# Windowed attention on one core: attend in 32x64 tiles of four stacked heads instead of 64x64 tiles of two

## The chip, the core and the metric

One NeuronCore of a Trainium2 chip runs the whole program in one launch. The metric is the device time of that launch in microseconds (us); the median of three runs is quoted. Engines are named as in the profile: PE (TensorE: matrix products, with PEld its weight loads), DVE (VectorE), ACT (ScalarE), POOL (GpSimd) and SP (SyncE, which here only issues DMAs).

## The reference

Two blocks work on `x` of 8 batches x 256 positions x 128 channels. The first block (linear attention, mixture of experts, a thresholded attention) is called the early part here. The change is in the second block's feed-forward place, a stack of six transformer layers with windowed attention; cut to what matters:

```python
DIM, DEPTH, HEADS, DIM_HEAD, WINDOW = 128, 6, 16, 64, 32
def attn_layer(x, Wqkv, qs, ksc, Wo):
    q, k, v = jnp.split(x @ Wqkv, 3, -1)          # each 256 x (16 heads x 64)
    q, k = l2norm(q) * qs, l2norm(k) * ksc        # then rotated by position
    out = local_attention(q, k, v)
    return out @ Wo
def local_attention(q, k, v):                     # 8 windows of 32 rows
    # keys and values of a window: the window before it and its own, 64 in all
    sim = einsum('bhwie,bhwje->bhwij', bq, bk2) * 8.0
    mask = (it < jb) | (it > jb + 32) | (jb == -1)
    attn = softmax(where(mask, -max, sim), -1)
    return einsum('bhwij,bhwje->bhwie', attn, bv2)
for i in range(DEPTH):
    x = attn_layer(shift_tokens(x), ...) + x
    x = ffn_layer(shift_tokens(x), ...) + x       # LayerNorm, gated gelu 128 -> 2 x 341 -> 128
```

## The kernel before

The six layers are 48 units `u` (layer `u // 8`, batch `u % 8`), each a generator `late(u)` in every engine's program. A table of slots per engine (`PE_AT`, `ACT_AT`, `DVE_AT`, `POOL_AT`, `SP_AT`) says at which slot after the start of its unit a step is written; units start 32 slots apart (`LATE_SPACING`), and `interleave` merges them. The tables set only the order in which instructions stand on an engine: engines run their lists in order and wait on semaphores. Five to seven units are in flight at once. The early part has tables of the same kind.

A unit has two chunks `c` of 128 positions. Its steps, with the lines of the profile:

- Projections: PE multiplies the shifted input by `Wqkv` in 12 pieces of 512 columns, 3 products each (L724 to L726, high and low parts in fp32r). ACT copies q and k to `raw` (L1063) and v to `vn` (L1080).
- Norm and rotation: ACT squares (L1071), DVE sums (L1528), ACT takes the root (L1137, L1138), POOL multiplies by the cosine (L1734) and adds (L1743), DVE multiplies by the sine (L1541) and normalises (L1549). PE transposes (L747), ACT copies to `qT` (L1091) and `kT` (L1097).
- Scores: `scores(c, half)` writes the mask with a bf16 product (L760), then 32 fp32 products in each half (L769) on 64-row, 32-column tiles: contraction over 64 head channels, 32 queries of one window as weights, 64 keys moving. One pair of PSUM banks, `s_pair`, serves both chunks in turn. In the trace each fp32 product is two load-and-multiply pairs, so a half is 64 records.
- Softmax: DVE takes the maximum and subtracts it (L1561, L1562), ACT the exponential (L1104), DVE sum, reciprocal and scaling (L1569 to L1571). PE transposes (L781), ACT copies to `pT` (L1111), so that the 64 keys of one head and window lie on 64 partitions, two heads on 128.
- Attend: `attend(c, half)` on 64x64 tiles (L799): 64 keys contracted, 64 value channels as weights, 32 queries moving, 128 records for each chunk. Results go to a second pair of banks, `o_pair`, which ACT copies to `oT` (L1119).
- Values: since a window needs the window before it, SP writes `vn` to HBM (L1883) and reads it back as `v2`, paired, each block twice (L1891).
- After it: output product `wo` (L882), residual (DVE L1609), LayerNorm (PE L887 and L891, ACT L1207 to L1213, DVE L1614 to L1624), the up products (L816 to L818), gelu (ACT L1129, with a table load of its own), gate (DVE L1578), down product (L904), residual (DVE L1631).

Three PSUM banks rotate among the remaining products, and a fourth holds tables of the rotation and small vectors.

## Time and profile before

| | |
|---|---|
| median of 3 runs | 1952.4 us (1951.92 to 1953.56) |
| span of the profiled execution | 1955.3 us |
| busy, of that span | PE 95%, PEld 80%, DVE 81%, ACT 81%, POOL 55% |
| mean granted TensorE clock | 0.979 of full speed |
| DMA | 212.35 MB, mean 109 GB/s |

The profile gives no time for the profiled execution beside its span. All times in the rows are of that one execution, 2.9 us above the median. The early part runs until about 430 us, and the 48 units follow, the first ones overlapped with its end. Within the units the work repeats, so one unit is read closely and multiplied; a row of the timeline gives the start, the time to the end of the last of its instructions, and how many were merged. The duration of a product holds its way through the array, so what it occupies is read from start to start.

### The profile page before, as it was taken

What the parts mean: (1) busy time and instruction counts of PE and PEld (TensorE: products, weight loads), DVE (VectorE), ACT (ScalarE), POOL (GpSimd) and SP (SyncE); (2) the same over time, 40 slices, a digit from 0 to 9 for tenths busy, and PEclk for the clock granted to TensorE, in tenths of its full rate; (3) what the DMA queues carried; (4) which work ended last, traced back from release to release, by engine and by line L of the source; (5) the groups of instructions that cost most, each with busy time, mean ns of one, the idle gap of its engine ahead of it and who ended that gap; (6) DMA issues with size and microseconds to landing.
All of it is one profiled execution on the core that took longest, in us unless ns stands there. A gap on an engine that the chain in (4) does not pass through costs nothing.

```text
span 1955.3 us, 77164 instructions
## 1 busy us (share of the span) xinstructions
PE 1866.8 (95%) x34029; PEld 1568.0 (80%) x34029; DVE 1587.6 (81%) x2234; ACT 1592.8 (81%) x2751; POOL 1069.6 (55%) x523
## 2 busy tenths in 40 slices
PE   6899999878999999999999999999999999999987
PEld 4788989856878888888878888887888888888876
DVE  3566765478898988989888998988898998989873
ACT  2578878667988888898988889897888889888864
POOL 3333222176565666657566666756575666657530
PEclk7999999979999999999999999999999999999998
DMA  6333322023335343353434443444434344333341
GB/s 175 121 127 124 105 80 66 2 72 96 105 99 156 96 132 111 105 150 95 124 100 130 123 125 108 112 122 122 113 103 132 97 137 129 105 115 94 101 105 29
DMA packets 134183, 212.35 MB, mean 109 GB/s; under 512 B 26871, under 2 KB 51034, under 8 KB 133850
## 3 DMA queue, kind: packets, MB, share of 16 engines
q1 hardware_dynamic: 133676, 207.36, 37.0%
q8 instruction: 269, 4.41, 1.0%
q14 instruction: 64, 0.52, 0.1%
q10 hardware_dynamic: 174, 0.05, 0.0%
HBM read 136.76 MB, written 70.60 MB: 106 GB/s over the span
## 4 chain that ended last, share of the span: by engine, by line
PE 86%; ACT 6%; DVE 5%; issue 3%; DMA 0%; ACTq 0%; SPq 0%; DVEq 0%
PE o_pair L799 9%; PE bank L747 9%; PE bank L882 9%; PE s_pair L769 7%; PE bank L724 7%; PE bank L725 6%; PE bank L726 6%; PE bank L781 4%; PE bank L649 4%; PE bank L904 3%; PE bank L816 2%; PE bank L817 2%; PE bank L818 2%; PE bank L887 2%; PE s_pair L760 1%
## 5 line engine op out<-in xcount | busy, mean ns | idle before, releaser
L1734 POOL TENSOR_TENSOR rt<-raw,rot 128x1024 f32<-128x1024 f32 x192 | 456.3, 2377 | 353.5 <-PE bank L747 328.8
L1743 POOL TENSOR_TENSOR rt<-rt,t 128x2048 f32<-128x2048 f32 x96 | 439.5, 4578 | 178.7 <-DVE t L1541 175.1
L724 PE MATMUL bank<-wqkv,xs 128*128 128x512 f32 x576 | 257.4, 447 | 11.6 <-ACT vn L1080 6.7
L1063 ACT ACTIVATE raw<-bank 128x512 f32<-128x512 f32 x384 | 223.2, 593 | 28.2 <-PE bank L726 14.9
L1528 DVE TENSOR_REDUCE bank<-t 128x32 f32<-128x2048 f32 x96 | 219.7, 2289 | 17.1 <-ACT t L1071 12.6
L726 PE MATMUL bank<-wqkv,xs 128*128 128x512 f32 x576 | 229.9, 399 | 0.0
L725 PE MATMUL bank<-wqkv,xs 128*128 128x512 f32 x576 | 229.8, 399 | 0.0
L747 PE MATMUL bank<-const,rt 128*128 128x128 f32 x1536 | 219.8, 281 | 9.5 <-issue 3.2
L799 PEld LDWEIGHTS o_pair<-pT,v 64*64 64x64 f32 x12288 | 196.2, 135 | 40.3 <-ACT oT L1119 17.6
L1541 DVE TENSOR_TENSOR t<-raw,bank 128x1024 f32<-128x1024 f32 x192 | 225.0, 1213 | 0.6
L1549 DVE TENSOR_TENSOR rt<-rt,bank 128x2048 f32<-128x2048 f32 x96 | 219.6, 2288 | 3.3
L799 PE MATMUL o_pair<-pT,v 64*64 64x32 f32 x12288 | 213.4, 220 | 6.5 <-issue 4.7
L1561 DVE TENSOR_REDUCE sm<-s_pair 128x16 f32<-128x1024 f32 x96 | 117.5, 1224 | 118.9 <-PE s_pair L769 118.2
L747 PEld LDWEIGHTS bank<-const,rt 128*128 128x128 f32 x1536 | 169.5, 142 | 38.6 <-ACT kT L1097 12.9
L1097 ACT ACTIVATE kT<-bank 128x512 f32<-128x512 f32 x192 | 109.2, 594 | 102.6 <-PE bank L747 100.6
L1071 ACT ACTIVATE t<-raw 128x2048 f32<-128x2048 f32 x96 | 184.0, 1917 | 10.4 <-POOL rt L1743 8.5
L769 PEld LDWEIGHTS s_pair<-kT,qT 64*32 64x32 f32 x12288 | 135.1, 106 | 52.4 <-issue 41.8
L882 PE MATMUL bank<-oT,wo 128*128 128x256 f32 x768 | 173.7, 379 | 0.4 <-DVE hh L1578 0.4
L769 PE MATMUL s_pair<-kT,qT 64*32 64x64 f32 x12288 | 167.1, 226 | 6.0 <-issue 6.0
L882 PEld LDWEIGHTS bank<-oT,wo 128*128 128x128 f32 x768 | 145.4, 190 | 22.0 <-DVE hh L1578 0.7
L1091 ACT ACTIVATE qT<-bank 128x512 f32<-128x512 f32 x192 | 113.9, 594 | 41.4 <-PE bank L747 40.3
L724 PEld LDWEIGHTS bank<-wqkv,xs 128*128 128x128 f32 x576 | 110.3, 191 | 34.7 <-ACT vn L1080 7.6
(403 smaller groups left out, 4157.5 us busy)
## 6 DMA issues: line engine op xcount, KB each, us to landing
v<-v_rows SPq DMA_DIRECT2D x288, 256.0 KB, 4.4
v_rows<-vn SPq DMA_DIRECT2D x192, 256.0 KB, 3.7
v<-v_rows SPq DMA_DIRECT2D x96, 192.0 KB, 3.2
w_parts<-wqkv SPq DMA_DIRECT2D x30, 512.0 KB, 3.8
wqkv<-w_parts SPq DMA_DIRECT2D x30, 512.0 KB, 4.1
wraw<-in_L_ffn_Wqkv_dram SPq DMA_DIRECT2D x36, 256.0 KB, 3.1
w_parts<-wqkv SPq DMA_DIRECT2D x10, 341.0 KB, 3.7
w<-w_parts SPq DMA_DIRECT2D x10, 341.0 KB, 5.7
```

Source lines behind the costliest of these rows:

```text
L724: pe.matmul(bank[:, :], hi, w[:, 0, :], start=True, stop=False)
L725: pe.matmul(bank[:, :], hi, w[:, 1, :], start=False, stop=False)
L726: return pe.matmul(bank[:, :], lo, w[:, 0, :], start=False, stop=True)
L747: e = pe.transpose(bank[:, i * P:(i + 1) * P], k.rt_r[c][:, at:at + P], k.ident)
L769: e = pe.matmul(k.s_pair[WIN * g:WIN * (g + 1), at:at + 2 * WIN], qT[rows, hp, WIN * g:WIN * (g + 1)], k.kT[rows, hp, k0:k0 + 2 * WIN], st ...
L799: e = pe.matmul(k.o_pair[cols, at:at + WIN], k.v2_r[c][rows, g, hp * DH:(hp + 1) * DH], k.pT_r[c][rows, hp, WIN * g:WIN * (g + 1)], start= ...
L882: e = pe.matmul(bank[:, 0:S], k.wo[:, n, :], k.oT_r[u % 2][:, n, :], start=(n == 0), stop=(n == INNER // P - 1))
L1063: act.activation(k.raw_r[c][:, n * 512:(n + 1) * 512], k.one.at["qk", j][:, :], ACT.Copy)\
L1528: dve.tensor_reduce(k.rn_p[c], heads(k.t2[:, :]), AX.X, ALU.add).then_inc(s["sq_sum"], 1)
L1541: e = dve.tensor_tensor(pairs(k.t2[:, part]), pairs(k.raw_r[c][:, part])[:, :, ::-1, :], sinv, ALU.mult)
L1734: e = pool.tensor_tensor(heads(k.rt_r[c][:, part]), heads(k.raw_r[c][:, part]), cosv, ALU.mult)
L1743: pool.tensor_tensor(k.rt_r[c][:, :], k.rt_r[c][:, :], k.t2[:, :], ALU.add).then_inc(s["rot_add"], 1)
```

## The change

**Attend.** Weights are now one block of 32 keys x 64 value channels, tiles have 32 rows x 64 columns, and four heads' key blocks are stacked on the four row groups, with two heads beside each other in columns: eight tiles. A value block of window `w` is loaded once and its product moves 64 queries, those of window `w` (the block is their own) and `w + 1` (the block is their previous one), accumulating in PSUM. Per unit there are 128 products as before (256 records), 224 of whose records move 64 columns and 32 move 32, all in one block after both chunks' softmax.

**Keys by block parity.** `kT` holds even blocks, then odd ones, so ACT's copy becomes two instructions of 256 columns. The two 32-key halves of a row of scores are placed by parity, `p` is laid out as window, head, key, and the mask and its spreading matrix follow.

**PSUM.** `so_pair[c]` takes the scores of chunk `c` and then half of the outputs of all 256 positions. Attend waits until DVE has read both pairs, and scores of the next unit wait until ACT has copied the outputs of that pair.

**DMA.** Values are stored in 2 writes per unit (4 before) and read in 8 reads of 128 KB (8 of 192 or 256 KB before). `wo` is loaded without rearranging channels.

**Slots.** All tables are new, also those of the early part, on slots an eighth as long.

```diff
 
-        def attend(c, half):
-            v = 2 * u + c
-            if half == 0:
-                if v:
-                    pe.wait_ge(s["oT"], v)
-                else:
-                    claim(k.banks[6:8])
-                pe.wait_ge(s["pT"], 2 * v + 2)
-                pe.wait_ge(s[f"v2_{c}"], pair_count(v))
-            for m in range(2 * half, 2 * half + 2):
-                for g in range(NW):
-                    for odd, cols in enumerate(halves):
-                        for r, rows in enumerate(halves):
-                            hp, at = 2 * m + odd, r * 512 + m * P + g * WIN
-                            e = pe.matmul(k.o_pair[cols, at:at + WIN], k.v2_r[c][rows, g, hp * DH:(hp + 1) * DH],
-                                          k.pT_r[c][rows, hp, WIN * g:WIN * (g + 1)], start=True, stop=True)
-            if half == 1:
-                e.then_inc(s["pe_o"], 1)
+        def attend():
+            pe.wait_ge(s["smax"], 2 * u + 2)
+            pe.wait_ge(s["pT"], 4 * u + 4)
+            pe.wait_ge(s[f"vq{u % 2}"], value_loads(u))
+            for w in range(NWS):
+                q0, n = w * WIN, 2 * WIN if w + 1 < NWS else WIN
+                for g2 in range(2):
+                    for hq in range(4):
+                        rows, pair = slice(32 * hq, 32 * (hq + 1)), k.so_pair[hq // 2]
+                        at = hq % 2 * 512 + g2 * S + q0
+                        for odd, cols in enumerate(halves):
+                            g = 2 * g2 + odd
+                            e = pe.matmul(pair[cols, at:at + n], k.vq_r[u % 2][rows, w, g, :],
+                                          k.pT[rows, 2 * g + w % 2, q0:q0 + n],
+                                          start=(w == 0 and g2 == 0), stop=(w == NWS - 1), skip_group_check=True)
+            e.then_inc(s["pe_o"], 1)
 
         def up(j):
...
-        def scores(c, half):
+        def scores(c):
             v = 2 * u + c
-            qT = k.qT_r[c]
-            if half == 0:
-                if v:
-                    pe.wait_ge(s["smax"], v)
-                else:
-                    claim(k.banks[4:6])
-                    pe.wait_ge(s["cst"], 1)
-                for r, rows in enumerate(halves):
-                    pe.matmul(k.s_pair[:, r * 512:(r + 1) * 512], k.spread_b[rows, :],
-                              k.mask_b[rows, min(c, 1), :].unsqueeze(1).to_broadcast([DH, HP, 2 * WIN]),
-                              start=True, stop=False, skip_group_check=True)
-                pe.wait_ge(s["qkT"], QK_EVACS * (v + 1))
-            for hp in range(4 * half, 4 * half + 4):
+            qT, pair = k.qT_r[c], k.so_pair[c]
+            if u == 0:
+                claim(k.banks[4 + 2 * c:6 + 2 * c])
+                pe.wait_ge(s["cst"], 1)
+            else:
+                pe.wait_ge(s["oT"], 2 * u - 1 + c)
+            for r, rows in enumerate(halves):
+                pe.matmul(pair[:, r * 512:(r + 1) * 512], k.spread_b[rows, min(c, 1), :],
+                          k.mask_b[rows, :].unsqueeze(1).to_broadcast([DH, HP, 2 * WIN]),
+                          start=True, stop=False, skip_group_check=True)
+            pe.wait_ge(s["qkT"], QK_EVACS * (v + 1))
+            for hp in range(HP):
                 for g in range(NW):
-                    k0 = c * P + g * WIN
+                    even, odd = (NW * c + g) // 2, NWS // 2 + (NW * c + g + 1) // 2
                     for r, rows in enumerate(halves):
                         at = r * 512 + hp * 2 * WIN
-                        e = pe.matmul(k.s_pair[WIN * g:WIN * (g + 1), at:at + 2 * WIN],
-                                      qT[rows, hp, WIN * g:WIN * (g + 1)], k.kT[rows, hp, k0:k0 + 2 * WIN],
+                        e = pe.matmul(pair[WIN * g:WIN * (g + 1), at:at + 2 * WIN],
+                                      qT[rows, hp, WIN * g:WIN * (g + 1)], k.kT[rows, hp, even:odd + 1:odd - even, :],
                                       start=False, stop=True, skip_group_check=True)
-            if half == 1:
-                e.then_inc(s["pe_s"], 1)
+            e.then_inc(s["pe_s"], 1)
 
         def transpose_p(c, n):
             v = 2 * u + c
+            p = k.p_r[c][:, :, :, :].rearrange("p w n j -> p w (n j)")
             bank = one_bank_for(("pT", 2 * v + n), "pT", 2 * v + n + 1)
...
-            act.activation(k.kT[:, 4 * (n - 2):4 * (n - 2) + 4, WIN + c * P:WIN + (c + 1) * P], src, ACT.Copy)\
-                .then_inc(s["qkT"], 1)
+            kT = k.kT[:, 4 * (n - 2):4 * (n - 2) + 4, :, :]
+            src = parity(src)
+            even, odd = 2 * c, NWS // 2 + 1 + 2 * c
+            for w, at in enumerate((even, odd)):
+                e = act.activation(kT[:, :, at:at + 2, :], src[:, :, w, :, :], ACT.Copy)
+            e.then_inc(s["qkT"], 1)
...
 
-        def evacuate_o(c):
-            v = 2 * u + c
-            act.wait_ge(s["pe_o"], v + 1)
-            if c == 0 and u >= 2:
+        def evacuate_o(n):
+            act.wait_ge(s["pe_o"], u + 1)
+            if n == 0 and u >= 2:
                 act.wait_ge(s["pe_wo"], u - 1)
-            act.activation(k.oT_r[u % 2][:, :, c * P:(c + 1) * P], k.o_pair[:, :].rearrange("p (n i) -> p n i", i=P),
+            act.activation(k.oT_r[u % 2][:, 4 * n:4 * n + 4, :], k.so_pair[n][:, :].rearrange("p (n i) -> p n i", i=S),
                            ACT.Copy).then_inc(s["oT"], 1)
...
-        def store_values(c, r):
+        def store_values(c):
+            if c == 0 and u >= 2:
+                sp.wait_ge(s[f"vq{u % 2}"], value_loads(u - 2))
+            sp.wait_ge(s["vn"], 4 * u + 2 * c + 2)
+            sp.dma_start(k.v_rows[u % 2, c * P:(c + 1) * P, :], k.vn_r[c][:, :, :, :].rearrange("p q g d -> p (q g d)"))\
+                .then_inc(s[f"st_v{c}"], 16)
+
+        def load_values(c, r):
+            if r == 0:
+                sp.wait_ge(s[f"st_v{c}"], 16 * (u + 1))
             if c == 0 and r == 0 and u >= 2:
-                for n in range(TC):
-                    sp.wait_ge(s[f"v2_{n}"], pair_count(2 * (u - 2) + n))
-            sp.wait_ge(s["vn"], 4 * u + 2 * c + r + 1)
-            sp.dma_start(k.v_rows[u % 2, c * P:(c + 1) * P, r, :], k.vn_r[c][:, r * 512:(r + 1) * 512])\
-                .then_inc(s[f"st_v{c}"], 16)
-
-        def pair_values(c, half):
-            v = 2 * u + c
-            if half == 0:
-                sp.wait_ge(s[f"st_v{c}"], 32 * (u + 1))
-                if u:
-                    sp.wait_ge(s["pe_o"], v - 1)
-                else:
-                    sp.wait_ge(s["zero_kv"], ZEROS)
-            g0 = 1 if c == 0 and half == 0 else 0
-            first = (NW * c + g0 - 1 + half) * WIN
-            for r in range(2):
-                at = 2 * WIN * r + WIN * half
-                src = k.v_rows[u % 2, first:first + (NW - g0) * WIN, r, :].rearrange("(g j) e -> j g e", j=WIN)
-                sp.dma_start(k.v2_r[c][at:at + WIN, g0:, :], src).then_inc(s[f"v2_{c}"], 16)
+                sp.wait_ge(s["pe_o"], u - 1)
```

The order on PE around the mask, scores and attend. In these rows a product stands once for its two records, `bank` is a rotating bank, L781 the transposes of probabilities, L904 the down product, L891 the LayerNorm variance. Before:

```order
L781 MATMUL bank<-const,p 128x128 x8
L904 MATMUL bank<-hh,w 128x256 x3
L760 MATMUL s_pair<-mask_b,spread_b 128x512 x2
L769 MATMUL s_pair<-kT,qT 32x64 x32
L891 MATMUL bank<-lnf,ones_d 128x256
L724 MATMUL bank<-wqkv,xs 128x512
L725 MATMUL bank<-wqkv,xs 128x512
L726 MATMUL bank<-wqkv,xs 128x512
L799 MATMUL o_pair<-pT,v 64x32 x64
L724 MATMUL bank<-wqkv,xs 128x512
```

After (L751 transposes q and k, L763 is the mask, L772 scores, L801 attend, L728 to L730 projections, L874 the variance):

```order
L751 MATMUL bank<-const,rt 128x128 x8
L801 MATMUL so_pair<-pT,vq 64x64 x112
L801 MATMUL so_pair<-pT,vq 64x32 x16
L728 MATMUL bank<-wqkv,xs 128x512
L729 MATMUL bank<-wqkv,xs 128x512
L730 MATMUL bank<-wqkv,xs 128x512
L728 MATMUL bank<-wqkv,xs 128x512
L729 MATMUL bank<-wqkv,xs 128x512
L730 MATMUL bank<-wqkv,xs 128x512
L874 MATMUL bank<-lnf,ones_d 128x256
L763 MATMUL so_pair<-mask_b,spread_b 128x512 x2
L772 MATMUL so_pair<-kT,qT 32x64 x64
```

Attend was three blocks per unit (32, 32 and 64 products), scores were four halves; now attend is one block of 128 and scores are two blocks of 64.

The order on DVE from the end of the second softmax sum. Before:

```order
L1569 TENSOR_REDUCE sm1<-p1 128x16
L1570 RECIPROCAL bank3<-sm1 128x16
L1571 TENSOR_TENSOR p1<-p1,bank3 128x2x8x64
L1614 TENSOR_TENSOR lnf<-xf0,bank0 128x256
L1561 TENSOR_REDUCE sm0<-s_pair 128x16
L1562 TENSOR_TENSOR p0<-s_pair,sm0 128x2x8x64
L1547 COPY bank3<-rn0 128x32
L1549 TENSOR_TENSOR rt0<-rt0,bank3 128x2048
L1528 TENSOR_REDUCE bank3<-t2 128x32
L1530 TENSOR_SCALAR rn1<-bank3 128x32
```

After (L1555 to L1557 is the softmax sum, L1600 the centring of LayerNorm, L1533 and L1535 normalise, L1514 and L1516 sum the squares `t2`, L1527 multiplies by the sine, L1606 to L1610 finish LayerNorm, L1547 takes the maximum of the next unit):

```order
L1555 TENSOR_REDUCE sm1<-p1 128x16
L1556 RECIPROCAL bank3<-sm1 128x16
L1557 TENSOR_TENSOR p1<-p1,bank3 128x1024
L1600 TENSOR_TENSOR lnf<-xf0,bank2 128x256
L1533 COPY bank3<-rn0 128x32
L1535 TENSOR_TENSOR rt0<-rt0,bank3 128x2048
L1514 TENSOR_REDUCE bank3<-t2 128x32
L1516 TENSOR_SCALAR rn1<-bank3 128x32
L1527 TENSOR_TENSOR t2<-raw1,bank3 128x1024 x2
L1606 SCALAR_TENSOR_TENSOR bank1<-lnf,cols,bank1 128x256
L1609 TENSOR_SCALAR hn<-bank1,cols 128x256
L1610 SCALAR_TENSOR_TENSOR hn<-bank1,cols,hn 128x256
```

The maximum of the next unit stood right behind the centring. Now normalise, the sum of squares, the rotation and the end of LayerNorm stand between them.

The order on ACT around the probabilities' copies. Before:

```order
L1207 ACTIVATE lnf<-lnf 128x256
L1063 ACTIVATE raw1<-bank0 128x512
L1063 ACTIVATE raw1<-bank1 128x512
L1071 ACTIVATE t2<-raw1 128x2048
L1111 ACTIVATE pT1<-bank2 128x512
L1111 ACTIVATE pT1<-bank0 128x512
L1119 ACTIVATE oT1<-o_pair 128x8x128
L1211 ACTIVATE lnf<-bank2,eps_ln 128x256
L1213 ACTIVATE bank2<-lnf 128x256
```

After (L1076 copies `qT`, L1100 `pT`, L1054 squares, L1086 copies `kT`, L1194 and L1198 belong to LayerNorm, L1107 copies `oT`):

```order
L1076 ACTIVATE qT1<-bank0 128x512
L1100 ACTIVATE pT<-bank1 128x4x128
L1100 ACTIVATE pT<-bank0 128x4x128
L1100 ACTIVATE pT<-bank1 128x4x128
L1100 ACTIVATE pT<-bank2 128x4x128
L1054 ACTIVATE t2<-raw1 128x2048
L1086 ACTIVATE kT<-bank0 128x4x64 x2
L1194 ACTIVATE lnf<-lnf 128x256
L1086 ACTIVATE kT<-bank1 128x4x64 x2
L1107 ACTIVATE oT0<-so_pair0 128x1024
```

The square of the second chunk stood ahead of that unit's pair of `pT` copies; now it stands behind four of them.

## Rows read from the trace of the kernel before

**Rows 1.** Busy time of each engine in two neighbouring stretches of 30.70 us (windows view).

```profile
core 0: us, PE busy (x) PEld busy (x) DVE busy (x) ACT busy (x) POOL busy (x), PEclk, DMA share, GB/s
1239.80:1270.50 30.70, 30.70 (x657) 25.56 (x652) 27.95 (x32) 27.38 (x47) 19.98 (x9) 1.00 0.44 117
1270.50:1301.20 30.70, 30.70 (x656) 25.57 (x649) 27.94 (x33) 27.38 (x47) 19.96 (x9) 1.00 0.36 101
```

**Rows 2.** Shares of the chain that ended last, by engine (the page).

```profile
PE 86%; ACT 6%; DVE 5%; issue 3%; DMA 0%; ACTq 0%; SPq 0%; DVEq 0%
```

**Rows 3.** Timeline of ACT: first exponential of the first and of the last unit.

```profile
429.77 1.04 ACT L1104 ACTIVATE p<-p 128x1024 f32<-128x1024 f32 x1
1900.93 1.04 ACT L1104 ACTIVATE p<-p 128x1024 f32<-128x1024 f32 x1
```

**Rows 4.** Timeline: where DVE and ACT sit idle within one undisturbed unit, idle in brackets.

```profile
1279.33 1.23 DVE L1561 TENSOR_REDUCE sm<-s_pair 128x16 f32<-128x1024 f32 x1 [2.04 <-PE s_pair L769]
1298.73 2.29 DVE L1528 TENSOR_REDUCE bank<-t 128x32 f32<-128x2048 f32 x1 [0.16 <-ACT t L1071]
1290.71 0.60 ACT L1091 ACTIVATE qT<-bank 128x512 f32<-128x512 f32 x1 [0.75 <-PE bank L747]
1294.26 1.09 ACT L1097 ACTIVATE kT<-bank 128x512 f32<-128x512 f32 x2 [1.61 <-PE bank L747]
```

**Rows 5.** Timeline of PE: two of the three attend blocks and what follows each.

```profile
1281.21 1.14 PE L799 MATMUL o_pair<-pT,v 64*64 64x32 f32 x64
1282.27 0.39 PE L816 MATMUL bank<-hn,w 128*128 128x256 f32 x1
1300.73 2.07 PE L799 MATMUL o_pair<-pT,v 64*64 64x32 f32 x128
1302.73 0.50 PE L724 MATMUL bank<-wqkv,xs 128*128 128x512 f32 x1
```

**Rows 6.** Timeline of PE: mask product, half a score block, and what follows.

```profile
1291.04 0.39 PE L760 MATMUL s_pair<-mask_b,spread_b 64*128 64x512 bf16 x2
1291.36 0.86 PE L769 MATMUL s_pair<-kT,qT 64*32 64x64 f32 x64
1292.17 0.67 PE L887 MATMUL bank<-xf,ones_d 128*128 128x256 f32 x2
```

**Rows 7.** Timeline of PE: a full-array product run, what follows, and column-tiled products.

```profile
1286.57 3.62 PE L882 MATMUL bank<-oT,wo 128*128 128x256 f32 x16
1290.03 1.08 PE L747 MATMUL bank<-const,rt 128*128 128x128 f32 x8
164.87 1.08 PE L568 MATMUL bank<-e_kp,e_vext 128*32 128x128 f32 x32
```

**Rows 8.** Groups by line: ACT copies of 512 and of 256 columns out of PSUM.

```profile
L1097 ACT ACTIVATE kT<-bank 128x512 f32<-128x512 f32 x192 | 109.2, 594 | 102.6 <-PE bank L747 100.6
L1031 ACT ACTIVATE e_hr<-bank 128x256 f32<-128x256 f32 x7 | 2.6, 372 | 0.0
```

**Rows 9.** Timeline of DVE: second softmax sum, LayerNorm centring, maximum, normalise.

```profile
1290.56 1.21 DVE L1569 TENSOR_REDUCE sm<-p 128x16 f32<-128x1024 f32 x1
1293.24 0.42 DVE L1614 TENSOR_TENSOR lnf<-xf,bank 128x256 f32<-128x256 f32 x1
1293.67 1.22 DVE L1561 TENSOR_REDUCE sm<-s_pair 128x16 f32<-128x1024 f32 x1
1296.07 0.18 DVE L1547 COPY bank<-rn 128x32 f32<-128x32 f32 x1
```

**Rows 10.** Timeline of ACT: square, transposed probabilities, table load, gelus.

```profile
1296.79 1.91 ACT L1071 ACTIVATE t<-raw 128x2048 f32<-128x2048 f32 x1
1298.61 1.06 ACT L1111 ACTIVATE pT<-bank 128x512 f32<-128x512 f32 x2
1282.34 1.28 ACT L1129 ACT_TABLE_LOAD   x1
1283.64 1.19 ACT L1129 ACTIVATE hh<-bank,cols 128x256 f32<-128x256 f32 x3
```

## What the change was predicted to do

> **What bounds the kernel now.** I read the busy time in two neighbouring stretches first. Each stretch of 30.70 us holds one unit's work: 656 or 657 multiplies, 32 or 33 DVE and 47 ACT instructions. PE is busy in all 30.70 us at the full clock, DVE in 27.95, ACT in 27.38, POOL in 19.98 [rows 1]. The chain that ended last agrees, with 86% on PE [rows 2]. The pace over the whole stack comes from the first exponential of the first and of the last unit: (1900.93 - 429.77) / 47 = 31.30 us for a unit [rows 3]. So an undisturbed unit takes 30.70 us by PE, and 0.60 us on average is disturbance, above all at the changes of layer, where DVE makes new rotation tables.
>
> How near the next engine is matters as much. In one unit DVE waited 2.04 us for PE's scores and 0.16 us for ACT's square, so DVE alone needs 30.70 - 2.20 = 28.5 us. ACT waited 0.75 and 1.61 us for transposes, so it needs 28.3 us [rows 4]. A saving on PE is worth its full size for 2.2 us a unit at most, and nothing after that.
>
> **Attend.** Two blocks of 64 records take 1282.27 - 1281.21 = 1.06 us each and one of 128 takes 1302.73 - 1300.73 = 2.00 us, 4.12 us a unit or 15.6 to 16.6 ns a record [rows 5]. What should a record cost in the new form? Sixteen records of 256 columns on the full array took 1290.03 - 1286.57 = 3.46 us, 216 ns each or 0.84 ns a column [rows 7]. A 32-column record thus streams for 27 ns. With four tiles side by side 16 ns a record is 64 ns a tile, so 37 ns beside the streaming are spent on weights and handing over. A score record streams 64 columns, 54 ns; 64 of them took 1292.17 - 1291.36 = 0.81 us, 12.7 ns each, on eight tiles 101 ns a tile, so 47 ns beside the streaming [rows 6]. The new record has the scores' 64 moving columns and eight tiles, and attend's 64-column weights. Streaming 54 plus 37 to 47 gives 91 to 101 ns a tile, over eight tiles 11.4 to 12.7 ns a record, for 256 records 2.9 to 3.2 us. I take 3.0, near the score row, whose tile count it shares: a gain of 1.1 us. The ends are streaming alone (256 x 54 / 8 = 1.7 us, gain 2.4) and the old price (4.1 us, no gain). A third bound lies above it: if only the four row groups work beside each other, see the rivals.
>
> **Scores.** The products are the same, but in two blocks, not four halves. Joining two attend blocks saved 2 x 1.06 - 2.00 = 0.12 us [rows 5], so two joins give 0.24, the lower bound. The half block's 12.7 ns a record holds entry and exit, while streaming needs 6.8, so up to 1 us is possible; I take 0.4. Between the blocks PE changes its tile shape seven times a unit now, and three times after; no row prices a change by itself, and the 0.12 us of a join is the nearest, so I put 0.3 us on four changes fewer (bounds 0 and 4 x 0.12 = 0.5). The mask product stays at 1291.36 - 1291.04 = 0.32 us [rows 6]. PE then needs 30.7 - 1.1 - 0.4 - 0.3 = 28.9 us a unit, with 27.0 and 30.4 as ends.
>
> **What ACT and DVE gain or lose.** Each of the four `kT` copies of 512 columns (594 ns) becomes two of 256. The nearest 256-column copy out of PSUM took 372 ns [rows 8], so a copy grows by at most 2 x 372 - 594 = 150 ns, a unit by 0.6 us, less where starts overlap. ACT needs 28.3 + 0.3 to 0.6, say 28.8 us. The value copies and `oT` copies move the same columns. DVE's softmax reads and writes the same 1024 elements in another order with runs of 32; I put nothing on it (bounds: nothing and, were runs to matter, some tenths). DVE stays at 28.5. POOL has 10 us to spare. Three engines now need 28.5 to 28.9 us: the bound is no longer one engine, it is their hand-overs.
>
> **The hand-overs.** Two are visible in the order. First, ACT's square of the second chunk stood ahead of the `pT` copies and now stands behind four of them, which wait for DVE's second softmax sum. DVE does centring and normalise after that sum and then needs this square. From the end of the sum: PE's last eight transposes, 1.0 us; the last copy, about 0.5 of the 1.06 for two, plus latency, 0.8; then the square, 1.91: 3.7 us [rows 10]. DVE meanwhile has 1293.67 - 1293.24 = 0.43 us of centring and 2.5 us of normalise (1296.07 to 1298.73 less the 0.16 idle) [rows 4, 9], so it waits 0.8 to 0.9 us where it waited 0.16. Second, gelu needs a table load of 1.28 us and 1.19 us for its three parts [rows 10], behind copies of projections, and DVE's gates come after only one maximum and subtraction (1296.07 - 1293.67 = 2.40 us [rows 9]); I put 0.2 us on it (0 to 0.7). DVE's 28.5 plus 0.9 plus 0.2 is 29.6 us. PE at 28.9 hides below that, which is why attend's price matters little unless it comes out above 3.7 us.
>
> The shared PSUM closes a ring: scores, both maxima, exponentials, both sums, transposes, attend, `oT` copy, scores. On DVE, all but five steps lies between the first maximum and the end of the second sum: centring 0.43, one normalise 2.5, one sum of squares 2.3 [rows 4, 9], one rotation (two passes over 1024, like the maximum's 1.22 each) and LayerNorm's end (three of about 0.45, like the centring), 9.0 us. That leaves 28.5 - 9.0 = 19.5 us. Then come PE's transposes and the copy (1.8), attend (3.0), two projections and the variance (eight records at about 0.22, 1.7 [rows 7]), and mask with scores (1.8): 27.8 us [rows 5, 6, 10]. It is shorter than 29.6, so it doesn't bind by this count, with 1.8 us in hand.
>
> **Values by DMA.** The value traffic halves, at a DMA share of 0.36 to 0.44 [rows 1]. DMA has no share in the chain [rows 2], so nothing is gained. The reads sit about a unit ahead of their attend in SP's list, and two buffers alternate by unit; I put 0 on them. The other loads that SP's list moved past them (weights of the next layer, `wo`) keep their order relative to their readers.
>
> **Sum.** A unit goes from 30.7 to 29.6 us undisturbed, and I leave the 0.60 us of disturbance: fewer transfers help, but DVE's layer tables now meet an engine without slack. 47 x 1.1 = 52 us. The early part's new tables and the ends of the stack I put at nothing (some us either way; no row prices them). On the profiled span that is 1955.3 - 52 = 1903, and 2.9 us less on the scale of the median: **1901 us**.
>
> **Rivals.**
> - Hand-overs vanish in queues that run ahead, and attend costs 2.5 us or less: a unit takes 28.6 us, 47 x 2.1 = 99 us, **1854 us**. For it: gaps in rows 4 were few. Against: three engines with 0.3 us of slack each. 17%.
> - Attend keeps its price of 16 ns a record (4.1 us), since weights and hand-over and not tiles set it. PE then needs 30.0, a unit 30.3 with hand-overs: 19 us, **1934 us**. For it: 37 of the 64 ns a tile are not streaming. 15%.
> - The ring binds, on the other side. Its place is the one wait of attend for both chunks and the wait of scores for the `oT` copy. Its 27.8 us plus waits inside it (residual behind `wo`, gates behind gelu, the copy queued behind the square) pass the present 30.7 when they reach 2.9 us; at 3.3 us the unit takes 31.1 and the kernel **1971 us**. Against: the waits I can name in it come to about 1. 8%.
> - Only row groups work side by side. What the rows show: 32 records of 128 columns on four column tiles took 1.08 us, 34 ns each, where streaming alone is 108 ns a tile [rows 7], so column tiles do overlap; and with two row groups an attend record at 27 ns of weights and 27 ns of streaming would cost 27 ns, not 16 [rows 5]. Were it so, 256 records at (27 + 54) / 4 ns would take 5.2 us, PE 31.1, the kernel **1971 us**. 3%. The Trainium skill says it, in "TensorE: Matmul & The Clock Gate", Part 3 on packing: a weight load overlaps a running multiply only where the row groups differ. By that rule as it stands the change loses; the trace of before disagrees with it for column tiles, so the row decides.
> - The change shifts nothing measurable, because another bound replaces attend exactly: **1952 us**. 2%.
>
> **How the numbers follow.** The forecast case (a unit of 29.1 to 30.1 us, 1877 to 1924 us) has 55%. The range goes from just above the first rival's value to just above the second's: 1855 to 1938 us, which leaves out the slow rivals, the null case and part of the first. Within 0.2% (4 us) is about what this measurement can't tell from no change. Faster is 55 + 17 + 15 = 87%, same 2%, slower 8 + 3 = 11%.
>
> **What would show it.** In the profile after: attend's block of 256 records from start to start (3.0 us; 4.1 or 5.2 by the rivals); the stretch of one unit near 29.6 us with DVE busy 28 of it, ACT about 28, and PE no longer waited on by DVE's maximum; DVE idle near 0.9 us before the sum of squares, released by ACT's square; the `kT` copies near 370 ns. A wait of scores on the `oT` copy of over 1 us each unit would mean that the ring binds. PE busy throughout at over 30 us would mean that attend was not made cheaper. The number is wrong if the disturbances grow, or if the early part moved by more than 10 us.

## The result and the profile after

The changed kernel takes **2130.65 us** (median of 4 runs, 2123.47 to 2138.64), the kernel before beside it 1952.16 us. The ratio is **1.090** (95% interval 1.086 to 1.094): 9% slower, where 1901 us were forecast and 1938 us was the upper end. The profiled execution took 2123.47 us, its span is 2122.1 us.

The page of the kernel after: busy time (share of the span) and instructions, the instruction queue, and the chain that ended last.

```profile
PE 1872.4 (88%) x34029; PEld 1544.8 (73%) x34029; DVE 1590.1 (75%) x2234; ACT 1594.3 (75%) x2943; POOL 1066.0 (50%) x521
q8 instruction: 269, 4.41, 0.9%
PE 58%; ACT 18%; DVE 12%; issue 11%; POOL 1%; DMA 0%; ACTq 0%; SPq 0%; DVEq 0%; POOLq 0%
```

PE is still 58% of the chain, but it was 86% [rows 2], and 11%, where it was 3%, are now "issue": time in which an engine stood still and waited for nothing that the profile shows. The first exponential of the first and of the last unit (timeline of ACT, kernel after) answer to [rows 3]:

```profile
463.97 1.04 ACT L1093 ACTIVATE p<-p 128x1024 f32<-128x1024 f32 x1
2069.63 1.06 ACT L1093 ACTIVATE p<-p 128x1024 f32<-128x1024 f32 x1
```

So the first unit comes 464.0 - 429.8 = 34 us later, and a unit takes (2069.6 - 464.0) / 47 = 34.16 us in place of 31.30, which is 134 us over the stack. What follows the last exponential is 2 us shorter. 34 + 134 - 2 is the 167 us between the two spans.

Where a unit's time went is read at attend. Timeline of PE, kernel after; it answers to [rows 5]:

```profile
1303.69 1.95 PE L801 MATMUL so_pair<-pT,vq 32*64 32x64 f32 x162
1307.73 1.55 PE L801 MATMUL so_pair<-pT,vq 32*64 32x64 f32 x94 [2.09 <-issue]
1309.20 0.80 PE L728 MATMUL bank<-wqkv,xs 128*128 128x512 f32 x1
...
1337.69 1.87 PE L801 MATMUL so_pair<-pT,vq 32*64 32x64 f32 x153
1341.37 1.51 PE L801 MATMUL so_pair<-pT,vq 32*64 32x64 f32 x103 [1.81 <-issue]
```

The records run at the forecast price, and then PE stands still for about 2 us in the middle of the block. In the next unit the gap is 9 records earlier. Behind it stands a second cost: the projection's first matmul takes 0.80 us. The windows view of the kernel after shows why, in its column PEclk (the granted clock, 1.00 is full; the columns are those of [rows 1]). The fourth row is the middle of the stack, the last one a unit that stays at the full clock:

```profile
1305.70:1307.70 2.00, 0.00 (x0) 0.00 (x0) 2.00 (x1) 1.17 (x5) 1.92 (x2) 1.00 0.00 0
1307.70:1309.30 1.60, 1.57 (x95) 1.51 (x94) 1.57 (x4) 0.00 (x0) 1.05 (x1) 0.61 0.05 10
1309.30:1311.10 1.80, 1.80 (x5) 1.42 (x6) 0.99 (x1) 1.02 (x1) 0.67 (x1) 0.50 0.00 0
700.00:1900.00 1200.00, 1088.63 (x22631) 884.76 (x22634) 984.83 (x1122) 963.34 (x1752) 697.56 (x281) 0.95 0.27 80
...
1117.20:1149.80 32.60, 30.04 (x646) 24.55 (x645) 28.06 (x32) 27.59 (x52) 19.97 (x8) 1.00 0.23 67
```

PE is empty for 2.00 us, and then the clock falls to 0.50. Added up over the stack's 47 units, the trace has 40 such stretches with 160 us at half clock (before: 4 with 17 us). A stretch at half clock gives back half of its length at most: 160 / 2 / 47 = 1.7 us a unit. Neighbouring units give the likelier size: with a gap of 1.6 to 1.8 us in both, one at the full clock takes 32.3 us (from 1598.8) and the next, with one such stretch, 33.7 (from 1631.1). With 40 stretches, some of them longer, in 47 units that is an estimate of 1.2 us a unit.

The waits view of the kernel after, 700 to 1900 us (35 units): waiter, releaser, us in total, times, longest.

```profile
PE so_pair L801 <- issue: 73.4, 37, 3.9
ACT oT L1107 <- PE so_pair L801: 80.3, 35, 4.4
DVE bank L1606 <- ACT bank L1200: 102.7, 36, 5.7
DVE hh L1564 <- ACT hh L1117: 53.0, 35, 1.9
DVE bank L1514 <- ACT t L1054: 31.0, 35, 1.1
```

The gap costs 73.4 / 35 = 2.1 us a unit. ACT waits for the end of attend 2.3 us a unit, and DVE then 2.9 us for ACT. The gap and the clock are 3.3 of the 34.16 us, 3.8 at most. That leaves 30.4 to 30.9 us where the forecast had 30.2. The unit at the full clock says the same: 32.6 us less its gap of 1.6 us is 31.0, no shorter than an undisturbed unit before (30.7).

Over 38 or 39 units in the middle of the stack, the mean time from each group of matmuls to the start of the next (us a unit, added up from the trace's records; waits and half clock are in it, a wait in the row of the group that stands ahead of it):

| | before | after | attend halved | attend cut in 3 |
|---|---|---|---|---|
| attend | 4.34 | 5.39 | 1.65 | 4.26 |
| projection products | 9.08 | 10.88 | 10.62 | 10.56 |
| scores | 3.34 | 3.50 | 3.39 | 3.94 |
| all else | 14.59 | 14.54 | 14.62 | 14.26 |
| unit | 31.35 | 34.31 | 30.28 | 33.02 |

The third and the fourth column are experiments `half` and `sp9` below.

### The profile page after: what moved, and what is told of

It is laid out like the page before. It is cut to its first block, busy times and chain, and to the rows that moved or that the text cites. A ratio compares the mean times of both kernels' runs of the same rounds, so it can differ in the third digit from the quotient of the medians.

```text
span 2122.1 us, 77095 instructions
## 1 busy us (share of the span) xinstructions
PE 1872.4 (88%) x34029; PEld 1544.8 (73%) x34029; DVE 1590.1 (75%) x2234; ACT 1594.3 (75%) x2943; POOL 1066.0 (50%) x521
## 4 chain that ended last, share of the span: by engine, by line
PE 58%; ACT 18%; DVE 12%; issue 11%; POOL 1%; DMA 0%; ACTq 0%; SPq 0%; DVEq 0%; POOLq 0%
PE so_pair L801 7%; PE bank L751 6%; PE bank L728 6%; PE bank L865 6%; PE bank L730 4%; PE bank L729 4%; PE bank L786 3%; PE so_pair L772 3%; PE bank L653 3%; ACT L911 3%; ACT L1117 3%; ACT raw L1046 2%; ACT t L1054 2%; DVE bank L1514 2%; DVE t L1527 2%
## 5 line engine op out<-in xcount | busy, mean ns | idle before, releaser
L728 PE MATMUL bank<-wqkv,xs 128*128 128x512 f32 x576 | 289.9, 503 | 32.7 <-ACT vn L1063 15.2
L801 PE MATMUL so_pair<-pT,vq 32*64 32x64 f32 (+1 forms) x12288 | 161.0, 238 | 102.7 <-issue 102.4
L1514 DVE TENSOR_REDUCE bank<-t 128x32 f32<-128x2048 f32 x96 | 219.7, 2289 | 42.0 <-ACT t L1054 42.0
L730 PE MATMUL bank<-wqkv,xs 128*128 128x512 f32 x576 | 243.8, 423 | 0.1
L729 PE MATMUL bank<-wqkv,xs 128*128 128x512 f32 x576 | 242.4, 421 | 0.0
L1535 DVE TENSOR_TENSOR rt<-rt,bank 128x2048 f32<-128x2048 f32 x96 | 219.7, 2288 | 19.8 <-POOL rt L1727 17.5
L801 PEld LDWEIGHTS so_pair<-pT,vq 32*64 32x64 f32 x12288 | 147.9, 137 | 118.3 <-issue 118.3
L1527 DVE TENSOR_TENSOR t<-raw,bank 128x1024 f32<-128x1024 f32 x192 | 224.8, 1212 | 0.6
L751 PE MATMUL bank<-const,rt 128*128 128x128 f32 x1536 | 205.5, 277 | 0.4 <-ACT raw L1046 0.4
L751 PEld LDWEIGHTS bank<-const,rt 128*128 128x128 f32 x1536 | 175.1, 141 | 28.1 <-ACT raw L1046 0.7
L728 PEld LDWEIGHTS bank<-wqkv,xs 128*128 128x128 f32 x576 | 115.5, 200 | 106.3 <-ACT vn L1063 35.1
L1054 ACT ACTIVATE t<-raw 128x2048 f32<-128x2048 f32 x96 | 183.0, 1906 | 6.5 <-POOL rt L1727 5.4
L1107 ACT ACTIVATE oT<-so_pair 128x1024 f32<-128x1024 f32 x96 | 98.4, 1025 | 118.5 <-PE so_pair L801 118.5
L772 PEld LDWEIGHTS so_pair<-kT,qT 64*32 64x32 f32 x12288 | 133.3, 108 | 33.5 <-issue 33.2
L772 PE MATMUL so_pair<-kT,qT 64*32 64x64 f32 x12288 | 150.9, 232 | 6.0 <-issue 5.9
L1606 DVE SCALAR_TENSOR_TENSOR bank<-lnf,cols,bank 128x256 f32<-128x256 f32 x48 | 23.5, 489 | 154.4 <-ACT bank L1200 154.4
L730 PEld LDWEIGHTS bank<-wqkv,xs 128*128 128x128 f32 x576 | 117.6, 204 | 29.7 <-issue 1.5
```

Of the source, the lines that this page charges most:

```text
L728: pe.matmul(bank[:, :], hi, w[:, 0, :], start=True, stop=False)
L729: pe.matmul(bank[:, :], hi, w[:, 1, :], start=False, stop=False)
L730: return pe.matmul(bank[:, :], lo, w[:, 0, :], start=False, stop=True)
L751: e = pe.transpose(bank[:, i * P:(i + 1) * P], k.rt_r[c][:, at:at + P], k.ident)
L772: e = pe.matmul(pair[WIN * g:WIN * (g + 1), at:at + 2 * WIN], qT[rows, hp, WIN * g:WIN * (g + 1)], k.kT[rows, hp, even:odd + 1:odd - even, :],
L801: e = pe.matmul(pair[cols, at:at + n], k.vq_r[u % 2][rows, w, g, :], k.pT[rows, 2 * g + w % 2, q0:q0 + n], start=(w == 0 and g2 == 0), sto ...
```

## What the gap is

**Theory (supply).** PE's instructions reach it in packets, and the new block uses them up faster than they come. Three numbers of the traces speak for it before any experiment:

- The instruction queue brought 269 packets of 16 KB. PE executed 34029 weight loads, 34029 matmuls and 863 semaphore instructions, 68921 in all: 269.2 times 256. So the queue carries PE's program, 256 instructions or 128 records to a packet.
- The shortest distance between two packets' starts is 3.2 to 3.4 us in every one of the 14 kernels of this study.
- Numbered from PE's first instruction, **each of the 50 gaps over 1 us inside attend ends at an instruction whose number leaves 193 or 194 when divided by 256**. A unit has 1299 to 1302 instructions, about 5 x 256 + 20: so the boundary drifts by some 20 instructions, 10 records, a unit, and the two timelines show 9.

If so, gap = 3.4 us less the time in which a packet is used up. In attend 128 records go in about 1.4 us, so the gap should be 2.0 us; it is 2.09 and 1.81 above. What repeats is the time from the first instruction of one packet to the first of the next across a gap: 3.1 to 3.8 us at three gaps in four, 3.5 in the middle. The packets themselves need not stand close: the one ahead of the gap's had come 3.3 to 19 us earlier. So the next packet seems to be sent for only when PE enters the one before it. Six of the 50 gaps are longer than this allows (over 4 us from packet to packet); why is open. The Trainium skill has the store behind this, in "Advanced Engine Details and Errata", section "ISA Cache": a cache line is 16 KB and 256 instructions, and there are "Only 2 cache lines!". The traces agree: if two packets were there at the start, the one that starts last before a gap is the one whose first instruction ends the gap, 2.3 to 2.9 us later, and no packet starts earlier than some 300 instructions ahead of its own, as it would with one line in use and one being filled. The same list of the Trainium skill gives TensorE 128 KB, which would be eight lines; nothing here shows a supply that far ahead.

**Rivals.** *Tile*: 32x64 tiles or four stacked heads are slow in themselves, or collide in a bank. *Hand-over*: the engines' order around attend is what costs, and the gap is only where it shows. *Early slots* for the 34 us.

## Experiments

**half**: one line, every second value window left out, so that attend has 128 records and its outputs lack half of their terms.

```diff
-            for w in range(NWS):
+            for w in range(0, NWS, 2):
```

> The changed kernel computing only the even value windows of attend (64 matmuls, 128 records in place of 256; the odd windows' part of every output is left out), all else as it is. Supply theory: 128 records take 1.4 us at 10.6 ns each, the hole behind them mostly goes (under 0.5 us a unit on average), the clock stays full; unit 34.2 - 1.35 (records) - 2.1 (hole) - up to 1.6 (clock), so 29.2 to 31 us, time 1900 to 1980. If only the records count: 34.2 - 1.35 = 32.8 us a unit, 2065 us. If another engine or the order of the hand-overs binds: 33.5 or more, over 2095 us.

One run: **1942.4 us** (before: 1953.4). Timeline of PE, and the same stretch of windows as above, then the page's packets:

```profile
1184.04 1.59 PE L801 MATMUL so_pair<-pT,vq 32*64 32x64 f32 x128
1185.56 0.51 PE L728 MATMUL bank<-wqkv,xs 128*128 128x512 f32 x1
...
700.00:1900.00 1200.00, 1126.79 (x20544) 897.08 (x20543) 1101.55 (x1263) 1073.63 (x1956) 768.97 (x307) 1.00 0.29 88
...
q8 instruction: 221, 3.62, 0.8%
```

A record in the new tiles costs 1.52 / 128 = 11.9 ns with entry and exit. Undisturbed units take 29.6 us and the mean is 30.24 (1890.3 less 469.1, over 47): taking 1.4 us of records out won 3.9 us. The clock is back at 1.00, with 2 half-clock stretches in place of 40. (27885 + 27885 + 863) / 256 = 221.2, again the packets. A pure count of records would have given 32.8 us a unit. So the records were not slow, which speaks against *tile*; and ACT's wait for attend fell from 80.3 us to 1.9 us in all. But with the missing records put back, 29.6 + 1.4 = 31.0 us, this is no faster than before either: what the whole block would take without its gap no run shows, and the rows leave 29.8 (PE's busy time, see below) to 31.0 us.

**dup**: the kernel **before**, its old 64x64 tiles, with the second chunk's attend issued twice.

```diff
-            for m in range(2 * half, 2 * half + 2):
+            for m in range(2 * (half % 2), 2 * (half % 2) + 2):
...
         yield from t.to("a11")
+        attend(1, 2)
+        attend(1, 3)
         attend(1, 1)
```

> The kernel before with the 64 attend matmuls of the second chunk issued twice in a row (same outputs; 256 records in one run in place of 128, old tile shape 64x64, at 15.6 ns a record in the trace of before). Supply theory: 256 records would take 4.0 us at their own price; a hole of 0.5 to 2 us appears in many of the blocks at a place that drifts by a fixed number of records a unit, a half clock behind some; unit 31.3 + 2.0 + 0.5 to 2.5, 33.8 to 35.8 us, time 2070 to 2165. Tile theory: no hole, exactly +2.0 us a unit, time 1952 + 96 = 2048 us or less.

One run: **2145.8 us**. Timeline of PE in two units:

```profile
1274.29 2.07 PE L799 MATMUL o_pair<-pT,v 64*64 64x32 f32 x128 [0.41 <-issue]
1278.31 0.83 PE L799 MATMUL o_pair<-pT,v 64*64 64x32 f32 x42 [1.95 <-issue]
...
1412.24 2.76 PE L799 MATMUL o_pair<-pT,v 64*64 64x32 f32 x174
1416.30 1.47 PE L799 MATMUL o_pair<-pT,v 64*64 64x32 f32 x82 [1.30 <-issue]
```

The old tiles get the gap as soon as 256 records stand in a row. 128 old records take 2.0 us, so the gap should be 3.4 - 2.0 = 1.4 us; 1.30 is seen in the fourth row. The first two rows have a smaller gap and a larger one 128 records apart: one packet. Of 43 gaps over 1 us in attend 42 lie at the same place, 193 or 194 of 256; the other stands early in the stack, at 461 us, where the kernel before has it too. The unit went from 31.3 to 35.2 us, 2.0 for the records and 1.9 for the rest, where *tile* gave 2.0 in all. This falsifies *tile*. The kernel before has the same gaps: after 600 us five of 1.0 to 2.8 us in attend and scores, all at the same place. It had few, because its attend stood in blocks of 64 and 128 records.

**split2**: the kernel after, attend in halves with two projection products between (`att0=1120, att1=1160`, `qk01` from 399 to 376).

```diff
+        def attend(part):
+            if part == 0:
                 pe.wait_ge(...)
-            for w in range(NWS):
+            for w in range(4 * part, 4 * (part + 1)):
```

> The changed kernel with the attend block in two halves of 128 records (windows 0 to 3, then 4 to 7) and two projection products (6 matmuls, 1.3 us) between them; the same products as before, only moved. Supply theory: TensorE's instructions come in packets, and a dense run of 256 records uses them up faster than they come; 1.3 us with only 12 instructions in the middle gives the supply time to catch up, so the 2.1 us hole shrinks by 1.3 us or goes, and with it the half clock behind it; a unit falls from 34.2 to 31.5 to 33 us and the whole by 60 to 130 us, to 2000 to 2070. Tile theory (32x64 tiles or the value loads of four stacked heads are slow in themselves, or the hole is a bank conflict within the block): holes stay, attend's sum per unit stays at 5.1 to 5.4 us, time 2130 plus up to 30, since the outputs are ready 1.3 us later.

**2085.1 us** (2079.2 to 2094.1, ratio to before 1.066). The waits view, 700 to 1900 us:

```profile
PE so_pair L772 <- issue: 21.6, 37, 1.1
PE so_pair L763 <- ACT oT L1110: 17.3, 35, 0.6
PE so_pair L802 <- issue: 16.6, 18, 2.3
```

The gap in attend fell from 73.4 to 16.6 us and the half clock from 160 to 61 us. A unit fell only from 34.16 to 33.37 us and the time is 15 us above the range that the supply theory had given. Part of the gap moved into the scores (21.6 us), and the scores now wait for ACT's output copy. Moving the same work removed the gap, so *tile* is out once more; but what the gap had cost was not given back.

**ho**: attend whole, the variance matmul straight behind it (`var` from 1424 to 1377), and ACT's logarithm and exponential ahead of its output copies (`rstd` from 1364 to 1356).

> The changed kernel with the attend block whole, but the variance matmul straight behind it and ScalarE's logarithm and exponential of the variance ahead of the copies of the outputs: it prices the hand-over of the LayerNorm alone. If the hand-overs bind (ScalarE's order is what costs): unit down by 1 to 2 us, time 2035 to 2085 us. Supply theory: the hole and half clock stay in TensorE's own stream, so at most 0.5 us a unit is won, 2105 to 2130 us.

**2138.9 us** (2134.1 to 2151.1), 8 us above the kernel after (2123.5 to 2138.6), which is not clear of noise; 9 us above the range of the supply theory, and far from that of the hand-overs. DVE's wait for the LayerNorm fell from 102.7 to 24.1 us in all, and in its place came a wait for the scores. Waits view, ACT and DVE:

```profile
ACT lnf L1198 <- PE bank L874: 110.9, 35, 5.7
DVE sm L1547 <- PE so_pair L772: 68.6, 35, 3.5
```

So the order alone wins nothing while the gap stands; one wait was exchanged for another.

**spread4, spread4_eo, spread_s**: attend in four blocks of 64 records with transposes or one product behind each, and ACT's order as in ho. The second has the old early slots too, the third also the first scores block 1.4 us later (`s0` from 912 to 940).

```diff
-PE_AT = dict(qk00=369, qk01=399, ... att=1120, ... var=1424, ...
+PE_AT = dict(qk00=356, qk01=360, ... att0=1106, att1=1113, att2=1125, att3=1129, ... var=1382, ...
-ACT_AT = dict(... rstd=1364, ...
+ACT_AT = dict(... rstd=1356, ...
```

> The changed kernel with the attend block in four blocks of 64 records (two windows each); between them stand four transposes, one product, and the variance matmul with one more product; ScalarE takes the logarithm and exponential of the variance ahead of the copies of the outputs. All work is kept, only moved. Supply theory: with 128 instructions at most in a run and 0.4 to 0.8 us of sparse work behind each, the hole of 2.1 us is spread out and mostly hidden; the half clock goes; the wait of the LayerNorm end behind the output copies (2.9 us a unit) goes. The run without half of attend gave 29.6 us a unit; with 1.4 us of records added back, 31.0 us, up to 32 if the scores block that follows still empties the supply; whole time 1965 to 2030 us. Tile theory: a block of 64 records would still hold its share of 2.1 us; attend 5 us a unit, unit 33.5 us or more, over 2095 us.

> The spread kernel with the early slots of the kernel before, as in the run early_old. The two effects lie in different parts of the time, so they should add: the spread kernel's time less 20 us (early_old won 20.2 us against 2130.65).

> The same as spread4_eo, with the first scores block two projection products (1.4 us) further from the last attend block. Supply theory: if the scores block still runs into an empty supply (holes inside it in the spread kernel), this wins up to 1 us a unit, 0 to 45 us below spread4_eo. If the supply has caught up by then, the softmax starts later for nothing: 0 to 30 us slower.

**2105.3, 2082.1 and 2104.8 us.** The first misses its forecast by 75 us, and its time, its mean unit of 33.7 us and its 5.0 us from attend to what follows are the numbers of the *tile* theory; the second and third met theirs. In spread4 gaps in attend fell to 23.7 us in all, 0.7 a unit, and half clock to 38 us, yet undisturbed units took 32.7 us. Another 1.1 us of the 5.0 are a wait behind the last block, as its first waits row tells:

```profile
PE so_pair L763 <- ACT oT L1110: 39.2, 35, 1.2
PE so_pair L802 <- issue: 23.7, 50, 2.2
```

In spread_s the scores' gaps went from 2.6 (spread4_eo) to 0.6 us in all, but PE waited 56.2 us for ACT's projection copies: the supply had caught up, and the softmax began later for nothing, as the second half of its expectation has it. The half clock rose too, from 55 to 126 us over the stack, so that up to 36 us may lie there; the run can't part the two.

**Second theory (loop).** The end of attend, ACT's output copy and the scores form a chain. Between the last `pT` copy and the output copy ACT has 3.3 us of its own work. In half that covers attend and 1.5 us are left: attend ended at 1185.56, the copy began at 1187.09. 128 records more, 1.4 us, would have fitted; the gap doesn't fit, and neither do products put between the blocks. Cutting attend removes the gap and moves attend's end as far. This is a count from rows; the run that tests it is sp9.

**sp6, sp7, sp8**: two blocks (128, 128: `att0=1120, att1=1129, qk00=360, qk01=370, var=1390`) and three blocks (64, 96, 96: `att0=1106, att1=1113, att2=1125, qk00=356, qk01=364, var=1382`), with one product behind the last block; sp8 is sp7 with the output projection moved between attend and the scores (`wo` from 1289 to 1161, `z_mid` from 1248 to 1074, `o1` from 1117 to 1103). All with old early slots and with ACT's order as in ho. They come from before the second theory.

> The changed kernel with old early slots and attend in two blocks of 128 records with one projection product between, then the variance matmul and one product ahead of the scores; ScalarE takes the LayerNorm's logarithm and exponential ahead of the output copies. In the four-block kernel (2082 us with these early slots) each cut cost 0.16 us, and the scores waited 1.16 us for the first output copy, since nothing stood behind the last block. Cover for that wait is back, two cuts fewer: a unit of 32.7 less 1.1 less 0.3, 31.3 us, if the supply holds: 2015 us. Supply theory: 776 instructions in 6.5 us from the first block to the end of the scores is denser than in the four-block kernel (8 us), so holes of 0.5 to 1 us a unit come back: 2035 to 2065 us.

> As sp6, but attend in three blocks (64, 96 and 96 records), the first behind the last transposes of the probabilities of the first chunk's windows and one group of transposes, so the dense stretch is 1 us longer in all. Expected 31.4 us a unit with fewer holes than sp6: 2020 to 2045 us, at or below sp6.

> As sp7, and the output projection (16 records of 128x256 in 3.3 us, the sparsest block in instructions) moved to stand between attend and the scores; VectorE's addition that follows it moved with it, and both output copies one after the other. Supply theory: the scores find a full supply; no hole there, the only waits left are for the output copies (2.0 us, covered by 1.7 us of other work). A unit of 30.5 to 31.2 us, 1975 to 2010 us. If something other than the supply and the copies holds the unit at 32 us or more, this stays at 2040 us or more.

**2109.6, 2088.2 and 2379.5 us**: sp6 and sp7 are 45 and 43 us above their ranges; in sp8 the second case of its expectation came, far above 2040. In sp6 and sp7 the wait for the output copy that I had thought covered was still there (39.1 us in 35 units and 42.7 us in 36). The timeline of ACT in sp7 shows the chain:

```profile
1276.38 0.66 ACT L1089 ACTIVATE kT<-bank 128x256 f32<-128x256 f32 x2
1279.03 0.47 ACT L1201 ACTIVATE lnf<-bank,eps_ln 128x256 f32<-128x256 f32 x1 [1.99 <-PE bank L877]
1279.54 0.39 ACT L1203 ACTIVATE bank<-lnf 128x256 f32<-128x256 f32 x1
1279.86 1.01 ACT L1110 ACTIVATE oT<-so_pair 128x1024 f32<-128x1024 f32 x1
```

ACT ran out of work 2 us before the variance came, and the output copy queued 0.8 us behind it. In sp8 the output projection needs a PSUM buffer that ACT frees only behind both output copies; PE waits there 77.5 us in 30 units, the softmax follows late, and a unit takes 40 us.

**sp9** tests the loop: sp7 with two places changed on ACT, the first projection copy ahead of the output copies and the LayerNorm's end behind the first of them.

```diff
-ACT_AT = dict(xs=193, qk00=342, ... rstd=1356, ...
+ACT_AT = dict(xs=193, qk00=332, ... rstd=1364, ...
```

> The kernel of sp7 (2088 us; clean units of 32.6 us, in which ScalarE idled 2.0 us for the variance matmul and the scores waited 1.1 us for the first output copy), with one change of order on ScalarE: it copies the first projection product of the next unit while the last attend block runs, then makes the first output copy, and only then the logarithm and exponential of the variance. The same work. Supply and loop theory (the end of attend, the output copy and the scores form a chain that ScalarE's own work must cover; cutting attend moved its end as far as the hole had): the copy comes 0.9 us earlier and 0.5 us of ScalarE's work fills the gap, so a clean unit is 31.2 to 31.7 us and the whole 2025 to 2055 us. If the chain through ScalarE is not what holds the clean units at 32.6 us, nothing moves: 2080 to 2095 us.

**2046.3 us** (2036.8 to 2048.1), within the range given, 42 us below sp7 with the same attend. Timeline of ACT:

```profile
1255.90 0.66 ACT L1089 ACTIVATE kT<-bank 128x256 f32<-128x256 f32 x2
1257.03 0.60 ACT L1049 ACTIVATE raw<-bank 128x512 f32<-128x512 f32 x1 [0.47 <-PE bank L730]
1258.19 1.03 ACT L1110 ACTIVATE oT<-so_pair 128x1024 f32<-128x1024 f32 x1 [0.56 <-PE so_pair L802]
```

ACT's idle time there is 1.0 us in place of 2.0, and no wait of the scores for the output copy is left in PE's list. The mean unit is 32.95 us (sp7: 33.87). The shortest units went from 32.4 to 31.5 us, as the loop has it, but the middle one of those at full clock only from 33.1 to 32.6, where 31.2 to 31.7 was expected. The half clock fell as well, from 79 to 27 us, which is worth 26 of the 42 us at most. So the loop is shown as a cause, by the wait that went and by the shortest units; its share of the 42 us is not. What remains on PE is supply:

```profile
PE so_pair L802 <- issue: 27.4, 32, 2.6
PE so_pair L772 <- issue: 18.5, 32, 1.0
```

That is 1.3 us a unit. sp9 is the best form of the change that I found, and at a ratio of 1.044 (1.040 to 1.048) it is still slower than the kernel before.

**early_old**: the kernel after with the early slot tables of before, times eight.

```diff
-PE_A = dict(ln_sq_a=79, ln_sd_a=79, ln_out_a=142, ...
+PE_A = dict(ln_sq_a=48, ln_sd_a=48, ln_out_a=112, ...
...
```

> The changed kernel with the slots of the part before the stack (tables PE_A, PE_B, ACT_A, ACT_B, DVE_A, DVE_B, POOL_B and their starts) set back to those of the kernel before, times eight; the stack's own tables stay. In the changed kernel the first exponential of the first unit came at 464.0 us, before at 429.8. If the new early slots are the cause of these 34 us: first exponential near 430, whole time 2130 - 34 = 2096 us, a unit of the stack unchanged at 34.2 us. If it is something that the stack's first units bring along (they overlap the end of the early part): first exponential stays near 464 and the time near 2130.

**2110.5 us** (2107.6 to 2112.6), 20 us won. Timeline of ACT, the first exponential:

```profile
442.65 1.06 ACT L1093 ACTIVATE p<-p 128x1024 f32<-128x1024 f32 x1
```

The early slots cost 464.0 - 442.7 = 21 of the 34 us. The other 13 are left with the old early slots, so they come with the stack: in early_old its first projection starts 8 us later than in the kernel before (378.8 against 371.0), and from there to the first exponential it is 5 us longer, with the first scores at slot 912 where 74 x 8 = 592 stood. That these two are the reason was not tried on the chip.

## Why the prediction was wrong, point by point

- **A record's price, 11.4 to 12.7 ns: right.** 11.9 ns in half. The rival in which only row groups work side by side is refuted: 256 records would have taken 5.2 us, and at full clock the block less its gap takes 3.1. (The 27 ns for weights in that rival stand in no row; the streaming alone, 256 x 54 / 4 ns = 3.5 us, refutes it too.) That attend did take 5.39 us is a coincidence of size.
- **Attend, 3.0 us a unit: the step that failed.** It multiplied a price read from blocks of 64 and 128 records by 256, as if PE could go on for any length, and put nothing on the supply of instructions. A packet's worth of records passes in 1.4 us and the next packet is there after some 3.4. Attend rose by 1.05 us (4.34 to 5.39) instead of falling by 1.1. The number of records did not change, nor did PE's 34029 matmuls and 34029 weight loads: 128 old records took 2.0 us in a block and were rarely caught, and the change spent the saving on waiting for the supply. The bounds (1.7 and 4.1 us) missed it, for no row of before that I had read shows a block longer than 128 records. Its rare gaps were visible: [rows 2] holds 3% "issue", which I didn't follow up.
- **The full clock was taken for granted.** Behind the gap it fell: some 1.2 us a unit, 1.7 at most.
- **Scores, -0.4 us: right for the records, not for the sum.** 128 records take 1.41 us in half; four halves of 0.80 had taken 3.2, two blocks 2.8. Smaller gaps, at most of the 70 blocks of the kernel after, took it back and more (3.50 against 3.34).
- **Fewer tile changes, -0.3 us: not seen, and PE's need was 0.9 us too low.** In an undisturbed unit of half (row below) PE is busy 28.48 us; with the missing 1.36 us of records it is 29.8, and in the kernel after's unit at full clock 30.0, against the forecast 28.9. So the forecast unit of 29.6 us was out of reach even without the gap. The order had been weighed only around attend and scores: the first projection product of a row of them takes 336 ns to the next start and the following ones 230, and in an undisturbed unit 8 of 12 take 336 ns or more to the next start, before 5 took 315 or more.

```profile
1166.70:1196.30 29.60, 28.48 (x519) 22.67 (x517) 27.84 (x32) 27.33 (x51) 19.99 (x8) 1.00 0.24 74
```

- **ACT and DVE: right in size.** The `kT` copies take 403 ns, 8 x 403 - 4 x 594 = 0.85 us more when each is taken alone and 0.2 to 0.7 in ACT's busy time. DVE's wait for the square is 31.0 / 35 = 0.89 us against 0.8 to 0.9. Its wait for the maximum's scores is gone. The gates' wait behind gelu was put at 0.2 (0 to 0.7) and is 53.0 / 35 = 1.5 us, since attend's delay reaches it through ACT; in half it is 0.5.
- **The ring: its chance of 8% was too low.** It was counted at 27.8 us with attend at 3.0. The gap alone used up its 1.8 us of slack, and cutting attend lengthened it again. Its named wait (scores on the output copy, over 1 us a unit) appeared in spread4, sp6 and sp7; the reordering that removed it in sp9 won 42 us, clock included. In the kernel after itself, PE's gap and clock come first.
- **The early part, "nothing": wrong by 34 us.** The text had said that over 10 us there would break the number. 21 of them are the new early slots.

Together: 34 us early, and in the stack 47 x (34.16 - 30.2) = 186 us above the forecast. The gap is 47 x 2.1 = 99 of them, the clock some 55 (80 at most), and what is left, some 32, is 0.7 us a unit by which PE's need had been put too low.

Two of the forecast's ends are also off by small sums that bear on nothing: streaming alone would save 256 x (12.7 - 6.8) ns = 1.5 us on the scores, not 1, and PE's lower end comes to 26.8 us with its own terms, not 27.0.

## What to carry to other kernels

A price per record holds only for blocks as long as those it was read from. Before making matmuls shorter or their blocks longer, divide PE's instructions by 256 and ask for every stretch of that many whether it lasts longer than the shortest distance between two instruction packets (3.3 us here); what is missing to it is a gap, and a gap may be followed by half clock. Add up the engine's need of a whole unit again too, not only around the change: here PE's need was 0.9 us higher than forecast, most of the 1.1 us that the change was to win. And when a gap is spread out, look at who waits for the block's end: work put in between is hidden only if that engine has other work meanwhile.

## What the runs showed of the hardware

- PE's instructions come 256 to a 16 KB packet, one packet in no less than 3.2 us in any of the 14 kernels. With two instructions to a record, 3.3 us a packet is 26 ns a record sustained, an estimate from these two numbers, where a record of the small tiles takes 11.9 ns.
- A gap of mostly 1.3 to 2.2 us (the longest 3.9) at one fixed place of the 256, in attend of both tile shapes and, shorter, in the scores. In the kernel after, the packet whose first instruction ends it starts 2.3 to 2.9 us earlier.
- After such gaps the granted clock falls to 0.50, the lower of the two levels (1.2 and 2.4 GHz): 40 times in the stack of the kernel after, twice in half. Not every gap is followed by one: 6 of 35 units with a gap of 1.6 us or more stayed at 1.00. The Trainium skill says in "TensorE: Matmul & The Clock Gate", Part 1, that the throttled state is the default and activity releases it; the traces agree in so far as the fall came behind idle time.
- Column tiles with 32 rows overlap as those of 64 rows do: 11.9 ns a record over eight tiles, where four row groups alone would give 54 / 4 = 13.5 ns by the estimate of the streaming alone, weights left out. The Trainium skill lets a weight load overlap a running multiply only where the row groups differ ("TensorE: Matmul & The Clock Gate", Part 3); the records disagree.
